# Cross attention and an expert mix on one core: one program on one memory map, with the expert weights prepared in attention's draining step

## The reference

```python
def attention(x, ctx):                       # per batch, 8 heads of 64
    q = softmax(Wq @ x, over the 64 channels) / 8
    k = softmax(Wk @ ctx, over the 1024 columns);  v = Wv @ ctx
    out = Wout @ ((v @ k.T) applied to q) + b_out
    return g * (out - mean(out)) * rsqrt(var(out) + 1e-5)      # over the 128 rows
x = x + attention(layernorm(x), ctx)
def mix(x):                                  # 64 experts of rank 16, the best 16 of each row
    scores = x @ Wr.T
    G = softmax of the 16 largest scores, 0 for the others
    return 2 * sum_k G[:, k] * (x @ A[k].T) @ B[k].T
x = x + mix(layernorm(x))
```

## Time and profile before

| what | us |
|---|---|
| median of 3 runs (1943.99 to 1944.69) | 1944.44 |
| the profiled execution, its own time | 1942.03 |
| its span, first to last instruction | 1940.3 |
| one attention step (PE's L680 at 1000.46 and at 1033.42) | 33.0 |
| two mix steps (the chain's PE L52 at 1215.28 and at 1262.02) | 46.7 |
| draining step 32 starts (PE's L680) | 1066.45 |
| first matmul of `hidden`, row block 0 | 1156.12 |
| first matmul of `hidden`, row block 1 | 1192.53 |

### The profile page before, as it was taken

The page is one execution under the profiler, slowest core; times in us unless marked ns, Lnnn a source line. Parts: engine busy times, 40 slices in busy tenths (PEclk is TensorE's granted clock), DMA queues, the critical chain, the costliest instruction groups (busy, mean ns, idle before and its releaser), DMA issues. The chain is left out here.

```text
span 1940.3 us, 27967 instructions
## 1 busy us (share of the span) xinstructions
PE 1827.7 (94%) x9820; PEld 1567.0 (81%) x9820; DVE 1492.3 (77%) x1987; ACT 1049.5 (54%) x1271; POOL 1138.4 (59%) x552
## 2 busy tenths in 40 slices
PE   5999999999999999999999636999999999999998
PEld 4888788888788888878887535999999999999997
DVE  6988888888888888898888366666777777777651
ACT  4788787878787878787887433222222222222210
POOL 4767676767676676767674442555555555555531
PEclk9999999999999999999999967999999999999999
DMA  3111111212121211111110443444444444444431
GB/s 121 55 66 55 64 66 54 76 54 76 54 76 54 74 56 65 65 65 65 65 44 22 147 141 103 158 157 158 152 161 164 162 152 151 153 161 155 162 128 65
DMA packets 90091, 194.92 MB, mean 100 GB/s; under 512 B 9344, under 2 KB 51968, under 8 KB 90048
## 3 DMA queue, kind: packets, MB, share of 16 engines
q1 hardware_dynamic: 76400, 170.76, 25.7%
q0 software_dynamic: 4608, 16.78, 2.9%
q10 hardware_dynamic: 9040, 6.82, 1.2%
HBM read 127.21 MB, written 67.11 MB: 100 GB/s over the span
## 5 line engine op out<-in xcount | busy, mean ns | idle before, releaser
L278 POOL TENSOR_TENSOR eq<-eq,q_inv 128x1024 f32<-128x1024 f32 x128 | 242.5, 1905 | 140.0 <-DVE q_inv L504 140.0
L282 POOL TENSOR_TENSOR kT_lo<-kT,kT_hi 128x1024 fp32r<-128x1024 f32 x128 | 304.5, 2402 | 0.7 <-ACT kT_hi L329 0.5
L1032 POOL TENSOR_TENSOR xT_lo<-work,xT_hi 128x1024 fp32r<-128x1024 f32 x32 | 76.5, 2389 | 349.9 <-ACT xT_hi L1090 349.9
L52 PE MATMUL ps<-w_ra_hi,xT_hi 128*128 128x384 f32 (+1 forms) x768 | 254.1, 331 | 5.6 <-DVE w_b_lo L1101 4.1
L53 PE MATMUL ps<-w_ra_lo,xT_hi 128*128 128x384 f32 (+1 forms) x768 | 253.6, 330 | 0.0
L54 PE MATMUL ps<-w_ra_hi,xT_lo 128*128 128x384 f32 (+1 forms) x768 | 253.5, 330 | 0.0
L52 PE MATMUL ps<-w_b_hi,hT_hi 128*128 128x512 f32 x512 | 205.4, 401 | 3.6 <-POOL hT_lo L1024 3.6
L347 ACT ACTIVATE ek<-ps,k_min 128x1024 f32<-128x1024 f32 x128 | 142.6, 1114 | 119.0 <-DVE k_min L508 119.0
L54 PE MATMUL ps<-w_b_hi,hT_lo 128*128 128x512 f32 x512 | 203.1, 397 | 0.0
L53 PE MATMUL ps<-w_b_lo,hT_hi 128*128 128x512 f32 x512 | 203.0, 397 | 0.0
L1037 POOL TENSOR_TENSOR rstd_c<-var_c,minus_half 128x32 f32<-128x32 f32 x32 | 174.5, 5452 | 34.3 <-DVE var_c L1234 34.3
(11 more groups left out here) (148 smaller groups left out, 4770.6 us busy)
## 6 DMA issues: line engine op xcount, KB each, us to landing
x_sb<-in_x SPq DMA_DIRECT2D x64, 512.0 KB, 4.3
ctx_hi<-in_ctx POOLq DMA_DIRECT2D x32, 512.0 KB, 3.7
ctx_sb<-in_ctx SPq DMA_DIRECT2D x32, 512.0 KB, 3.4
attention_out<-o_sb SPq DMA_DIRECT2D x32, 512.0 KB, 2.6
o_sb<-attention_out SPq DMA_DIRECT2D x32, 512.0 KB, 4.6
x_turn<-x_blk SPq DMA_DIRECT2D x32, 512.0 KB, 2.6
work<-x_turn SPq DMA_DIRECT2D x128, 128.0 KB, 3.0
h_turn<-h_blk SPq DMA_DIRECT2D x32, 512.0 KB, 3.6
```

What stands on the lines that cost most here:

```text
L52: pe.matmul(out, stat_hi, mov_hi, start=first, stop=False)
L278: pool.tensor_tensor(v, v, per_row(q_inv[:, i, :], 2 * HEADS, DH), ALU.mult).then_inc(q_normed, 1)
L282: pool.tensor_tensor(kT_lo[:, i % 2, :, :], kT[:, i % 2, :, :], kT_hi[:, i % 2, :, :].bitcast(F32), ALU.subtract).then_inc(kT_lo_ready, 1)
```

## The change

**One program.** The two stages become one function and one block. No engine meets the others at a jump between the stages; each goes from attention's last instructions straight into `mix_step`.

**A drawn memory map.** Every large SBUF tensor gets a fixed address, and the mix's tensors lie on addresses that attention has finished with. Waits are added where one takes over from the other. There are five raw buffers (`out_sb`, `hg`, `h_blk`, `h_raw`, `x2_2`) in place of three.

**Weight jobs in step 32.** Jobs 0 to 8 take the nine places that projections would have in the ring (`PLACES`). Beside them stand the row preparation of the blocks 0 and 1; that of block 0 begins in step 31 already. B's jobs 9 to 16 all stand in mix step 0, behind `hidden`. The mix starts at step 0; the steps -3 to -1 are gone. The squares of the blocks 0 to 2 go to SBUF (`sq_sb`) and no longer to PSUM.

**B in row order by DMA.** In each attention step SP issues two transfers, each of one expert's B (1024 rows of 16 numbers, 64 bytes) from HBM to a tensor `b_turned` in HBM with one row of 1024 numbers (4 KB) for each output channel. The raw loads of the B jobs read 128 columns of it, and `order_rows` is gone.

The places, the raw buffers, the wait in `wait_slot`, and SP's part:

```diff
+PLACES = ["Q0", "K0", "Q1", "K1", "Q2", "K2", "Q3", "K3", "C0"]
+RAW_SLOT = [0, 1, 2, 3, 0, 1, 2, 3, 0, 3, 4, 0, 3, 4, 0, 3, 4]
...
+                if edge and s - back == BATCHES and RING[n] in PLACES:
+                    eng.wait_ge(w_lo_ready, PLACES.index(RING[n]) + 1)
+                    return
...
+        raw = [out_sb[:, :], hg[:, :], h_blk[:, :], h_raw[:, :], x2[2][:, :]]
...
+            else:
+                dst = dst.rearrange("p (j c) -> p j c", j=NCH)
+                src = b_dram.rearrange("(p j) c -> p j c", j=NCH)[:, :, (n - A_JOBS) * P:(n - A_JOBS + 1) * P]
+            eng.dma_start(dst, src).then_inc(raw_loaded[RAW_SLOT[n]], 16)
...
+            def place_b(s):
+                dst = b_dram.rearrange("d (s e r) -> s e d r", e=2, r=RANK)
+                src = B.rearrange("(s e) d r -> s e d r", e=2)
+                for e in range(2):
+                    sp.dma_start(dst[s, e], src[s, e]).then_inc(b_placed, 16)
+            def first_rows():
+                sp.wait_ge(o_stored[0], 16 * (LAST // 2))
+                load_o(0, 0)
+                sp.wait_ge(k_made, CH * LAST)
+                sp.wait_ge(q_made, 4 * LAST)
+                for n in range(4):
+                    load_raw(sp, n)
+                sp.wait_ge(xn_ready, BATCHES)
+                load_rows(0, 0)
+                load_rows(1, 1)
+                sp.wait_ge(ctx_lo_ready, LAST)
+                sp.wait_ge(c_turned, LAST)
+                load_o(1, 1)
...
+                if edge and s == LAST:
+                    first_rows()
+                if on("K", s, edge):
+                    place_b(s)
...
+                if edge and s == BATCHES:
+                    load_o(2, 0)
+                    turn_rows(0)
```

POOL, in attention's step:

```diff
+                    if edge and s == BATCHES:
+                        invert_rows(0)
                     keys_lo(s - 1, 2)
                     keys_lo(s - 1, 3)
+                if edge and s == LAST:
+                    invert_blocks(0)
+                if edge and s == BATCHES:
+                    invert_blocks(1)
+                    scale_blocks(1)
+                    rows_lo(0)
```

ACT:

```diff
+            def weight_hi(n):
+                act.wait_ge(w_turned, n + 1)
+                act.copy(weight_part(0, n), weight_slot(n)).then_inc(w_hi_ready, 1)
+                later = [k for k in range(n + 1, WEIGHT_JOBS) if RAW_SLOT[k] == RAW_SLOT[n]]
+                if later:
+                    load_raw(act, later[0])
...
+            def mix_step(t, par, tri):
+                if due(t, -1):
+                    hidden_hi(t - 1)
+                if isinstance(t, int) and t == 0:
+                    square_rows(2)
+                if due(t, 0):
+                    gate_exps(t)
+                if due(t, 1):
+                    norm_rows(t + 1, (tri + 1) % 3)
+                if isinstance(t, int) and t == 0:
+                    for n in range(A_JOBS, A_JOBS + 4):
+                        weight_hi(n)
+                    rows_hi(1)
+                    for n in range(A_JOBS + 4, WEIGHT_JOBS):
+                        weight_hi(n)
+                if due(t, 3):
+                    square_rows(t + 3)
+                if due(t, 1) and not (isinstance(t, int) and t == 0):
+                    rows_hi(t + 1)
...
+            def last_step(s, par):
+                keys_copy(LAST, 0)
+                weight_hi(0)
+                keys_hi(LAST, 0)
+                keys_copy(LAST, 1)
+                output(s - 2, par)
+                weight_hi(1)
+                keys_hi(LAST, 1)
+                keys_copy(LAST, 2)
+                weight_hi(2)
+                keys_hi(LAST, 2)
+                keys_copy(LAST, 3)
+                keys_hi(LAST, 3)
+                square_rows(1)
+                weight_hi(3)
+                query_hi(LAST, 1 - par, 0)
+                norm_rows(0, 0)
+                weight_hi(4)
+                weighted_hi(LAST)
+                weight_hi(5)
+                folded_hi(LAST)
+                act.wait_ge(b_placed, 16 * EXPERTS)
+                load_raw(act, A_JOBS + 1)
+                query_hi(LAST, 1 - par, 1)
+                weight_hi(6)
+                query_hi(LAST, 1 - par, 2)
+                rows_hi(0)
+                weight_hi(7)
+                query_hi(LAST, 1 - par, 3)
+                weight_hi(8)
```

DVE, first in attention's step, then in the mix:

```diff
+                if edge and s == LAST:
+                    block_rows(0, 0)
                 if X_:
                     stats_x(s + 1, 1 - par, 1)
                 if Q:
                     sum_queries(s, par, 0)
                 if K:
                     min_keys(s, par, 1)
+                if edge and s == LAST:
+                    sum_squares(0)
                 if Q:
                     max_queries(s, 2)
                 if X_:
                     mean_x(s + 1)
+                if edge and s == LAST:
+                    variance(0)
```

```diff
+            def mix_step(t, par, tri):
+                b, p, v, u = t + 1, 1 - par, t + 2, t + 3
+                if due(t, -2):
+                    add_out(t - 2, (tri + 1) % 3)
+                if due(t, 1):
+                    residual(b, p, (tri + 1) % 3)
+                if isinstance(t, int) and t == 0:
+                    sum_squares(2)
+                if due(t, 0):
+                    top_scores(t)
+                if due(t, 1):
+                    shift_rows(b)
+                if due(t, 0):
+                    gates(t)
+                    gate_hidden(t, 0)
+                if isinstance(t, int) and t == 0:
+                    variance(2)
+                if due(t, 1):
+                    turn_rows(b)
+                if due(t, 0):
+                    gate_hidden(t, 1)
+                    gate_hidden(t, 2)
+                    turn_hidden(t)
+                if isinstance(t, int) and t == 0:
+                    for n in range(A_JOBS, WEIGHT_JOBS):
+                        weight_lo(n)
+                if due(t, 2):
+                    turn_back(v, par)
+                if due(t, 3):
+                    block_rows(u, p)
+                    sum_squares(u)
+                    variance(u)
...
+            def last_step(par):
+                turn_back(0, 0)
+                weight_lo(0)
+                sum_queries(LAST, 1 - par, 3)
+                invert_sums(LAST, 3)
+                invert_keys(LAST, 1 - par)
+                residual(0, 0, 0)
+                weight_lo(1)
+                block_rows(1, 1)
+                weight_lo(2)
+                shift_rows(0)
+                sum_squares(1)
+                weight_lo(3)
+                query_lo(LAST, 1 - par, 0)
+                turn_rows(0)
+                variance(1)
+                weight_lo(4)
+                weighted_lo(LAST)
+                weight_lo(5)
+                folded_lo(LAST)
+                query_lo(LAST, 1 - par, 1)
+                weight_lo(6)
+                query_lo(LAST, 1 - par, 2)
+                weight_lo(7)
+                turn_back(1, 1)
+                query_lo(LAST, 1 - par, 3)
+                weight_lo(8)
+                block_rows(2, 0)
```

PE:

```diff
+            def turn_a(n, s):
+                wait_slot(pe, PLACES[n], s, True)
+                weight_rows(n)
+            def turn_b(n):
+                if n == A_JOBS:
+                    pe.wait_ge(o_copied, BATCHES)
+                if n == A_JOBS + 1:
+                    pe.wait_ge(var_ready, 3)
+                if n > A_JOBS + 1:
+                    pe.wait_ge(w_lo_ready, n - 1)
+                weight_rows(n)
...
+            def mix_step(t, par, tri):
+                if due(t, 0):
+                    if isinstance(t, int) and t == 0:
+                        pe.wait_ge(w_lo_ready, A_JOBS)
+                    pe.wait_ge(x_lo_ready, t + 1)
+                    wait_for(pe, h_gated, 3 * t)
+                    hidden(0)
+                    hidden(1)
+                    if isinstance(t, int) and t == 0:
+                        average(2)
+                    hidden(2)
+                if isinstance(t, int) and t == 0:
+                    for n in range(A_JOBS, WEIGHT_JOBS):
+                        turn_b(n)
...
+            def last_step(s, par):
+                turn_keys(s, par, 0, True)
+                turn_a(0, s)
+                turn_keys(s, par, 1, True)
+                add_output(s - 2, 3)
+                turn_a(1, s)
+                turn_keys(s, par, 2, True)
+                turn_a(2, s)
+                add_weighted(LAST, 0)
+                turn_keys(s, par, 3, True)
+                add_weighted(LAST, 1)
+                turn_a(3, s)
+                turn_a(4, s)
+                turn_query(s, par, 0, True)
+                add_weighted(LAST, 2)
+                average(1)
+                add_weighted(LAST, 3)
+                turn_a(5, s)
+                fold(s, True)
+                turn_query(s, par, 1, True)
+                turn_a(6, s)
+                turn_query(s, par, 2, True)
+                add_output(LAST, 0)
+                turn_a(7, s)
```

(6 more changed lines are left out.)

931 lines of the change are left out of this document (425 added, 506 removed).

## The result

The changed kernel takes 1886.58 us (median of 4 runs, 1885.05 to 1887.64) against 1944.22 (4 runs): ratio 0.9703, 95% interval 0.9687 to 0.9720. The forecast was 1897, range 1888 to 1909: the gain is there, 58 us, and 10 us larger than forecast, outside the range. The profiled execution took 1887.64 us, 1885.9 of them its span.

The account below looks back on a forecast made before the run. PE paces middle attention steps; the 126.1 us passage between stages is a chain with no engine full. 126.1 - 77.6 = 48.5 won, 1.3 lost: 47.2 off 1942.0 gives 1894.8, plus 2.4 for the median: 1897, range 1888 to 1909.

Parts of the forecast that it names:

- What doesn't change: Both loops: same instructions and order on PE, DVE, ACT and POOL, so the same 23.4 us a mix step.
- a loop with a new length: Sign that the forecast is wrong altogether: a loop of new length with the same instructions; no size given.
- Step 32: Attention's draining step with nine A jobs and rows added: `hidden` of block 0 starts 35.8 us after its start.
- It stays there: PE's clock in step 32: full before at 23.2 busy of 31.6 us, and to stay full with more work.
- rival A: Step 32 crowded by A jobs, in-order waits adding up: +8 us, 1905 (1899 to 1921); chance 0.14.
- Block 0's `hidden`: First block's `hidden` after step 32: 12.0 us at full clock in place of 13.6, done at 47.8.
- B jobs: Eight jobs after block 0's `hidden`, two PSUM pairs alternating: two rounds at 5.1, two at 6.0, plus 2.0; 24.2 us.
- Tail: Behind the last low part: 5.0 us, then 0.6 for the small matmul; `hidden` of block 1 starts at 77.6.
- Step 31: Attention step before step 32: DVE's added row work delays PE by 1.3 us, between 0 and 2.9.
- Placing B: B's transfers in attention steps: 0.030 to 0.104 us a packet, 3.8 to 13.3 us a step, costing nothing up to 0.14.
- C: Rival: placing B paces all 32 attention steps from 0.22 us a packet; at 0.3 some 2205 us; chance 0.05.
- B's sign: Rival B, raw loads pacing the B jobs (+8 us, 1905; chance 0.08), shows as transposes waiting for DMA from `b_turned`.

Follow-up runs that it names:

- second measurement: The changed kernel run once more, unaltered, on the same chip as two later versions: 1890.19 us, ratio 0.9723 to the kernel before.
- the one reordering tried: Changed kernel with the low part of A job 1 ahead of block 0's residual in DVE's list of step 32: 1889.61 us, ratio 0.9728.
- after_moved_32: Changed kernel with its whole memory map 32 bytes later: 1889.6 us, ratio 0.9724 to the kernel before.
- after_placed_twice: Changed kernel with B placed in row order a second time, into another DRAM tensor: 1888.96 us, ratio 0.9721 to the kernel before.
- after_b_three_slots: Changed kernel with three pairs of PSUM banks (places) for the eight B jobs in place of two: 1884.43 us, ratio 0.9699 to the kernel before.

## Why the forecast was wrong, point by point

- **The failed step is "What doesn't change"**: "Both loops have the same instructions in the same order on PE, DVE, ACT and POOL; start and end too", and from it "the same 23.4 us a mix step". The premise holds and the conclusion doesn't. I took a matmul's length to depend on its shape and the clock alone; it depends on where its two operands lie, too. It is 10.8 of 747.8 us, and shown from both sides: 128 bytes bring the kernel before down by 10.7 us, and 128 bytes the other way bring the changed one's same part up by 7.3, with five of eight pairs of B tiles moved. The forecast named a loop with a new length as what would make it wrong altogether; it had a new map of the memory before its eyes and gave that no case. Had the loop kept its length, the sum would have been 3.6 us too short for the profiled execution, while the median would have come out at 1897: a hit in the number that owed something to luck, since the 2.4 us added for the median didn't show again (the profiled execution was 1.1 us above it).
- **Step 32: 37.9 against 35.8.** The lists were sized nearly rightly: DVE 32.7 busy with the collisions in it (I had 30.8 and 3.3), PE 31.5 (32). "It stays there", of the clock, was wrong for this execution: the mean fell to 0.95, and eight transposes took 1.91 us soon after 2.29 us of waiting. The second measurement has the same wait and no fall, and 36.80 us. Up to the end of that wait the two are alike (22.38 and 22.35 us from the start of step 32), so 1.1 of the 2.1 us are the fall:

```profile
1070.91:1107.71 36.80, 30.11 (x205) 25.97 (x206) 32.64 (x36) 27.24 (x30) 25.29 (x11) 1.00 0.55 172
```

  The other 1.0 us was not isolated by a run. The residual took 2.90 us and the `shift` 1.85 beside POOL, as said; the one reordering tried didn't help. What the second measurement does show is idle time: DVE waited 3.9 us in all for ACT's results, where the forecast left its list of 34.1 us only 1.3 us to the ninth low part at 35.4. That would be rival A's in-order waits at a small size.
- **Block 0's `hidden`**: 12.08 for 12.0.
- **B jobs: 25.4 against 24.2.** The mechanism was right, places and not loads. The term that was off is when the transposes become 1.97 us: I took 8.5 us after `hidden`'s end, they did so 5.2 us after it, so only one round was a short one (5.2 us) and the others took 6.1.
- **Tail 5.3 for 5.6; step 32 starts 1.8 us later, for 1.3.** Step 31, to which the forecast gave the 1.3, took 0.7 more (33.74 for 33.03). Another 0.4 was there at step 2 (76.93 for 76.51), and 0.7 came in the 29 steps between (957.60 for 956.91), which the forecast had put at nothing. The placing isn't the cause of that: placed twice it is 957.54. What is stays open.
- **Placing B: nothing**, right; the two bounds of a packet's price, 0.030 and 0.104 us, were both too high, by factors from 2 to 12. By the Trainium skill's rule ("DMA: Bandwidth & Descriptors", Specifications) that transfers under 512 bytes are read, modified and written I had allowed a doubling to 0.21 us; 64-byte packets at 0.009 to 0.013 us don't bear such a price out here. Whether the rule itself holds for them, no run shows.
- Rivals A and C didn't come at their size. B's sign, a wait of the transposes for `b_turned`, came at 1.26 us in the second measurement of the changed kernel, 1.58 in `after_moved_32` and 0.41 in `after_placed_twice`, against the forecast of 8 us; it grew to 5.37 once a third place took its cover away.

## What to carry to other kernels

A new memory map is an edit to every instruction that reads through it, also where the instructions and their order stay. When PE runs matmul behind matmul without a wait, read the spacing of two neighbours of one form, work out the distance of moving and stationary operand modulo 256, and try a pad that makes it 0: here 128 bytes were worth 10.7 us of 1943. And where a chain with no full engine is shortened, look behind it first: the third place uncovered the loads, the added buffers uncovered a wait in ScalarE's list, and with that gone too the B jobs were 5.7 us shorter; the last 8.6 us, on PE's order, brought nothing. Whether each edit would pay alone was tried for the third place only.

## What the runs showed of the hardware that I had not expected

- **Distance.** 176 against 173 ns for 384 columns, 233 against 228 for 512, none for 320 (147 ns). It is there in every step read, to 0.04 us in a run of 36 matmuls, whatever the other engines do. The Trainium skill ("TensorE: Matmul & The Clock Gate", Step-by-step: what each phase is for) states that TensorE reads the moving and the stationary operand through ports of their own and that loading the next weights takes no read bandwidth from the running matmul. That is not enough to foretell the time here: with nothing else changed, the relative place of the two operands decides 1.7% of it at 384 columns and 2.3% at 512. Whether it is the load of the weights that meets the running matmul, and in which port or bank, no run here shows.
- **The start is not the same each time.** Between 25 and 45 us the changed kernel's granted clock was 0.91 in one execution and 0.66 in the other; attention's step 1 started at 43.45 and 46.14, and step 32 at 1068.27 and 1070.91. This later start is most of the 3.1 us between the two spans (1885.9 and 1889.0). The clock alone doesn't explain it: `after_b_three_slots` had 0.66 there too, and its step 1 started at 44.72. It is a reason to compare stretches, and not only totals:

```profile
25.00:45.00 20.00, 13.27 (x57) 9.87 (x56) 16.36 (x19) 10.78 (x16) 9.31 (x6) 0.91 0.20 64
```

```profile
25.00:45.00 20.00, 13.26 (x44) 9.56 (x43) 15.23 (x18) 8.88 (x14) 7.73 (x5) 0.66 0.09 26
```

- **Small packets are cheap beside a loop that doesn't need the queues**: 0.009 to 0.013 us for 64 bytes, where 512-byte packets in a busy stretch had 0.030.
